# In-degrees counted from sorted destinations, and one histogram beside the aggregations of a graph network

## Time and profile before

| | us |
|---|---|
| median of 3 runs | 5533.93 (5531.75 to 5538.64) |
| span of the profiled execution | 6224.7 |
| set-up | 0 to 61 |
| input stage | 61 to 430 |
| first aggregation | 430 to 1609 |
| first dense stage | 1609 to 1726 |
| rows stage | 1726 to 1864 |
| second aggregation | 1864 to 3033 |
| second dense stage | 3033 to 3152 |
| mixing stage | 3152 to 3507 |
| dispatch and expert stage | 3507 to 4200 |
| the second layer | 4200 to 6225 |

### The profile page before, as it was taken

How to read it: one execution, slowest core, us unless ns; L and a number is a source line. 1 busy time by engine, 2 the same in 40 slices (tenths; PEclk the granted TensorE clock), 3 DMA queues, 4 the chain that set the end, 5 groups by cost and what they waited for, 6 DMA issues and landing times. The chain is left out here.

```text
span 6224.7 us, 73410 instructions
## 1 busy us (share of the span) xinstructions
PE 3894.4 (63%) x17328; PEld 2978.0 (48%) x17328; DVE 3162.7 (51%) x8327; ACT 2366.6 (38%) x6680; POOL 4026.6 (65%) x3591
## 2 busy tenths in 40 slices
PE   5645555555654555555756329987775877777763
PEld 4543343433453343333445228875554655556542
DVE  5544444444614444444578776535472435544566
ACT  2225566656425665666444213333441111111112
POOL 4876666666576666666588767875666666666523
PEclk7757777777776777777856569998997888889886
DMA  9774333333373333333378747868552112212235
GB/s 246 142 155 134 90 91 91 90 90 92 69 145 90 92 90 90 91 91 91 67 150 169 187 113 161 172 111 249 125 119 76 39 39 49 54 35 56 53 128 168
DMA packets 699733, 683.06 MB, mean 110 GB/s; under 512 B 96160, under 2 KB 623742, under 8 KB 698644
## 3 DMA queue, kind: packets, MB, share of 16 engines
q0 software_dynamic: 243744, 307.67, 25.2%
q1 hardware_dynamic: 440688, 345.82, 18.3%
q10 hardware_dynamic: 14980, 25.87, 1.2%
HBM read 475.03 MB, written 203.98 MB: 109 GB/s over the span
## 5 line engine op out<-in xcount | busy, mean ns | idle before, releaser
L729 POOL DMA_INDIRECT a_msg<-h_d,conv_src x1564 | 1479.0, 946 | 812.2 <-issue 437.0
L779 PE MATMUL a_part<-a_msg,a_pick 128*128 x3328 | 1226.9, 527 | 1046.6 <-issue 608.4
L621 POOL DMA_INDIRECT sums_d<-ss_total,ss_row_i x784 | 1276.5, 1628 | 452.1 <-issue 282.9
L779 PEld LDWEIGHTS a_part<-a_msg,a_pick 128*128 128x128 f32 x3328 | 819.5, 264 | 1415.1 <-issue 1271.6
L756 DVE TENSOR_TENSOR acc<-acc,a_part 128x256 f32 x1664 | 700.4, 421 | 1255.1 <-PE a_part L779 621.9
L3631 POOL DMA_INDIRECT es_edge<-gat_rows_d,el_idx x824 | 802.7, 974 | 473.4 <-issue 223.8
L743 DVE TENSOR_SCALAR a_pick<-ramp,conv_rel,conv_weight 128x128 f32<-128x128 f32 x1680 | 581.2, 347 | 0.2
L2581 ACT ACTIVATE cb_lent<-e_hp,e_b1c 128x256 f32<-128x256 f32 (+1 forms) x400 | 154.6, 469 | 1008.4 <-DMA gm_x<-in_L_gnn_z_out,gm_out_i 497.4
L2621 PE MATMUL e_yp<-cb_lent 128*128 128x256 f32 (+1 forms) x1568 | 417.0, 426 | 51.0 <-ACTq L2583 45.1
L2621 PEld LDWEIGHTS e_yp<-cb_lent 128*128 128x128 f32 (+1 forms) x1568 | 344.1, 221 | 116.7 <-ACTq L2583 47.1
L828 ACT ACTIVATE a1c_one_lo<-ramp,a1c_digits 128x128 bf16<-128x128 f32 x928 | 278.0, 387 | 311.0 <-remote 310.4
(11 more groups left out here) (557 smaller groups left out, 6851.0 us busy)
## 6 DMA issues: line engine op xcount, KB each, us to landing
ss_key_row<-keys_d SPq DMA_DIRECT2D x98, 512.0 KB
ss_pay<-in_edge_attr SPq DMA_DIRECT2D x97, 512.0 KB
a_msg<-h_d,conv_src POOLq DMA_INDIRECT x1564
experts_d<-cb_lent SPq DMA_DIRECT2D x96, 256.0 KB
cb_lent<-experts_d SPq DMA_DIRECT2D x30, 512.0 KB
y_rows_d<-node_h SPq DMA_DIRECT2D x28, 512.0 KB
e_xs<-y_rows_d SPq DMA_DIRECT2D x56, 256.0 KB
out_rows_d<-e_ys SPq DMA_DIRECT2D x56, 256.0 KB
```

The source lines that it names most:

```text
L621: nc.gpsimd.indirect_dma_start(self.out_d[q], bass.IndirectOffsetOnAxis(ap=self.row_i[n % 4][:, j:j + 1], axis=0), self.total[n % 4][:, j, ...
L729: nc.gpsimd.indirect_dma_start(msg[:, ds((j + PART) % SLOTS * C, C)], None, table, bass.IndirectOffsetOnAxis(ap=src_i[:, j:j + 1], axis=0) ...
L779: nc.tensor.matmul(part[b % BANKS][:, 0:C], pick[s % AHEAD][:], msg[:, ds(slot, C)], start=True, stop=True).then_inc(summed, 1)
```

## The change

The histogram of the first layer's destinations leaves the aggregations; the other one is counted in 128 batches of 8 columns, one per window, from a single set of buffers. PE's two numbers per step are packed into one, which it takes apart by masking. The in-degrees are found in the rows stage by the new class `InDegrees`: the sorted destinations lie as 112 rows of 896 keys; for each tile of 128 nodes, DVE marks which row holds a node's end (`choose`), PE brings that row's keys in two halves (`find`), and DVE counts the keys below the node (`count`); at the end a shift by one node and a subtraction give the degrees (`place`, `shift`). Each aggregation issues six of the edge sum's scatters behind its last gather. The dense stages serve seven groups, four of them behind blocks 1, 4, 7 and 10, and the mixing stage 20. `list_dst_digits` goes. `scatter_chunks` is `scatter` with its limits in chunks.

```diff
@@ EdgeOrder.set_up
-                nc.vector.tensor_scalar(self.chunk_row[:, :, 0], chunk_from[:], (SLOTS - 1) * C, None, ALU.bitwise_and)
-                nc.vector.tensor_scalar(self.chunk_row[:, :, 1], chunk_from[:], (PART * C).bit_length() - 1, None,
+                nc.vector.tensor_scalar(self.chunk_row[:, 0, :], chunk_from[:], (SLOTS - 1) * C, None, ALU.bitwise_and)
+                nc.vector.tensor_scalar(self.chunk_row[:, 1, :], chunk_from[:], (PART * C).bit_length() - 1, None,
                                         ALU.logical_shift_right)
+                dve.drain()
+                nc.vector.tensor_tensor(self.chunk_row[:, 0, :], self.chunk_row[:, 0, :], self.chunk_row[:, 1, :],
+                                        ALU.add)
@@ aggregate
         @block.scalar
         def _(act):
-            def window(n, i, h):
-                counts.scalar_batch(act, h % 2, i * 2 + h // 2)
-            over_windows(act, W, window)
+            with act.Fori(0, WINDOWS) as n:
+                counts.scalar_batch(act, n)
...
+            sums.scatter_chunks(pool, group * sums.B, group * sums.B + AHEAD_CHUNKS)
...
-            regs = [pe.alloc_register(f"{tag}_{what}{b}") for b in range(K) for what in ("slot", "in")]
+            regs = [pe.alloc_register(f"{tag}_chunk{b}") for b in range(K)]
-                pe.reg_load(regs, chunk_row[0:1, ds(n * K, K), :])
-                slots = [pe.snap(r, min_val=0, max_val=(SLOTS - 1) * C) for r in regs[0::2]]
-                parts = [pe.snap(r, min_val=1, max_val=PARTS) for r in regs[1::2]]
+                pe.reg_load(regs, chunk_row[0:1, 0, ds(n * K, K)])
+                where = [pe.snap(r, min_val=1, max_val=(SLOTS - 1) * C + PARTS) for r in regs]
...
-                    pe.wait_ge(landed, parts[b] & 255)
-                    slot = slots[b]
+                    pe.wait_ge(landed, where[b] & 255)
+                    slot = pe.snap(where[b] & (SLOTS - 1) * C, min_val=0, max_val=(SLOTS - 1) * C)
...
-                counts.tensor_batch(pe, h % 2, i * 2 + h // 2)
+                counts.tensor_batch(pe, n)
@@ CountBeside
-    BATCHES = 64
+    BATCHES = 128
...
-        self.digits = [sb(f"digits{q}", [P, 2, B], F32) for q, B in enumerate(self.cols)]
-        self.one_lo = [sb(f"one_lo{q}", [P, B, P]) for q, B in enumerate(self.cols)]
-        self.one_hi = [sb(f"one_hi{q}", [P, B, NHI]) for q, B in enumerate(self.cols)]
+        self.digits = sb("digits", [P, 2, B], F32)
+        self.one_lo, self.one_hi = sb("one_lo", [P, B, P]), sb("one_hi", [P, B, NHI])
@@ new
+class InDegrees:
+    ROW = EdgeOrder.PER * P
+    ROWS = CE // EdgeOrder.PER
+    HALF = ROW // 2
...
+    def load(self, sp):
+        rows = self.keys_d[:, 1, :].rearrange("(p b) e -> p b e", b=EdgeOrder.PER)
+        keys = self.keys[0:self.ROWS, :].rearrange("p (b e) -> p b e", e=P)
+        sp.dma_start(keys, rows).then_inc(self.keys_in, 16)
+        sp.wait_ge(self.next_ready, 1)
+        sp.dma_start(self.next[0:self.ROWS - 1, :], rows[1:self.ROWS, 0, 0:2]).then_inc(self.keys_in, 16)
+    def prepare(self, dve):
...
+        dve.wait_ge(self.keys_in, 32)
+        nc.vector.tensor_tensor(self.first[0:R], self.first[0:R], self.keys[0:R, 0:1], ALU.min)
+        nc.vector.tensor_copy(self.whole[0:R], self.keys[0:R])
+        dve.drain()
+        for to, of in ((self.firsts, self.first), (self.nexts, self.next)):
+            nc.vector.tensor_scalar(to[0:R], ramp[0:R, 0:NT], -float(P), of[0:R, 0:1], ALU.mult, ALU.add)
+        for digit, by, op in ((0, 127, ALU.bitwise_and), (1, (NHI - 1) * P, ALU.bitwise_and)):
+            keys = self.keys.bitcast(I32)
+            nc.vector.tensor_scalar(keys[0:R, :], self.whole[0:R], by, None, op)
+            dve.drain()
+            nc.vector.tensor_copy(self.digits[digit][0:R, 0:self.ROW], keys[0:R, :])
+            dve.drain()
...
+    def choose(self, dve, t):
+        R, ramp, behind = self.ROWS, self.k.ramp[0:self.ROWS, :], self.behind[t % 2]
+        self.nc.vector.tensor_scalar(behind[0:R], ramp, self.nexts[0:R, t:t + 1], None, ALU.is_le)
+        dve.drain()
+        if t >= 2:
+            dve.wait_ge(self.offered, 2 * t - 2)
+        self.nc.vector.scalar_tensor_tensor(self.chosen[t % 2][0:R], ramp, self.firsts[0:R, t:t + 1], behind[0:R],
+                                            ALU.is_gt, ALU.mult).then_inc(self.chose, 1)
+    def find(self, pe, t):
+        R, H = self.ROWS, self.HALF
+        pe.wait_ge(self.chose, t + 1)
+        for half in (0, 1):
+            if t:
+                pe.wait_ge(self.taken, 2 * t + half - 1)
+            for digit in (0, 1):
+                mm = self.nc.tensor.matmul(self.found[half][:, 0:H + half], self.chosen[t % 2][0:R, :],
+                                           self.digits[digit][0:R, half * H:half * H + H + half],
+                                           start=digit == 0, stop=digit == 1)
+            mm.then_inc(self.offered, 1)
+    def count(self, dve, t):
+        nc, H = self.nc, self.HALF
+        for half in (0, 1):
+            dve.wait_ge(self.offered, 2 * t + half + 1)
+            if half:
+                nc.vector.tensor_copy(self.at[:, 1, t:t + 1], self.found[1][:, H:H + 1])
+            nc.vector.tensor_scalar(self.junk[:], self.found[half][:, 0:H], self.node[:, t:t + 1], 0.0, ALU.is_lt, ALU.add,
+                                    accum_out=self.counted[:, half, t:t + 1])
+            dve.drain().then_inc(self.taken, 1)
...
@@ constants
-MIX_GROUPS = 22
+MIX_GROUPS = 20
-DENSE_GROUPS = 6
+DENSE_GROUPS = 7
+AHEAD_CHUNKS = 6
@@ dense_and_norms
         def served(n):
-            return all_groups[n * early // blocks:(n + 1) * early // blocks]
+            return all_groups[n // 3:n // 3 + 1] if n % 3 == 1 and n // 3 < early else ()
...
-            sums.scatter(pool, first - 2, first + DENSE_GROUPS - 2)
+            sums.scatter_chunks(pool, (first - 2) * sums.B + AHEAD_CHUNKS, (first + DENSE_GROUPS - 2) * sums.B)
...
-                if n == 5:
-                    sums.make_equal(dve, first + 2, first + 2)
-                    sums.choose_rows(dve, first, first)
-                if n == 10:
-                    sums.make_equal(dve, first + 3, first + 3)
-                    sums.choose_rows(dve, first + 1, first + 1)
+                if n % 3 == 0 and 0 < n <= 3 * early:
+                    g = all_groups[n // 3 - 1]
+                    sums.make_equal(dve, g + 2, g + 2)
+                    sums.choose_rows(dve, g, g)
...
-                sums.make_equal(dve, g + 1, g + 1)
-                if n == 0:
-                    sums.choose_rows(dve, g - 1, g - 1)
+                sums.make_equal(dve, g + 2, g + 2)
                 sums.choose_rows(dve, g, g)
-            sums.make_equal(dve, first + DENSE_GROUPS, first + DENSE_GROUPS)
@@ rows_from_channels
         @block.vector
         def _(dve):
-            for g in range(first, first + ROWS_GROUPS):
+            degrees.prepare(dve)
+            degrees.choose(dve, 0)
+            def tile(t, b, r):
+                if t + 1 < REAL_T:
+                    degrees.choose(dve, t + 1)
+                degrees.count(dve, t)
+            def serve(g):
                 sums.make_equal(dve, g + 1, g + 1)
                 sums.choose_rows(dve, g - 1, g - 1)
+            each_tile(tile, serve)
+            degrees.place(dve)
...
+                degrees.find(pe, t)
...
+            degrees.shift(pe)
...
+            degrees.load(sp)
```

More of the change, by code:

```diff
@@ L606, in scatter, with scatter_chunks @@
     def scatter(self, pool, first, last):
+        self.scatter_chunks(pool, max(first, 0) * self.B, last * self.B)
+    def scatter_chunks(self, pool, first, last):
         nc, B, Q = self.nc, self.B, self.Q
-        for chunk in range(max(first, 0) * B, last * B):
+        for chunk in range(first, last):
             n, j = divmod(chunk, B)
@@ L656, in _, with aggregate @@
             nc.vector.tensor_tensor(start[:], tile_start[:], within[:], ALU.add)
-def aggregate(k, tag, table, src_i, rel, weight, first_row, chunk_row, freed_row, acc, counts, first_batch, clear=None):
+def aggregate(k, tag, table, src_i, rel, weight, first_row, chunk_row, freed_row, acc, counts, first_batch, sums, group,
+              clear=None):
     nc = k.nc
@@ L780, in window, with __init__ @@
                                      ).then_inc(summed, 1)
[L781 removed]
+                counts.tensor_batch(pe, n)
             for n in range(WINDOWS):
[L783 removed]
+                window(n)
             counts.tensor_end(pe)
 class CountBeside:
[L789 to L793 removed]
+    BATCHES = 128
+    def __init__(self, k, lo, hi, count):
+        self.k, self.nc, self.lists, self.count = k, k.nc, (lo, hi), count
+        self.cols = lo.shape[1] // self.BATCHES
     def open(self, c, tag, first):
[L797 removed]
+        nc, B = self.nc, self.cols
         self.first = first
@@ L833, in scalar_batch @@
             nc.scalar.activation(whole, whole, ACT.Relu, bias=self.k.ones[:, 0:1], scale=-1.0)
```

(38 more changed lines are left out.)

119 lines of the change are left out of this document (74 added, 45 removed).

## The result

The changed kernel takes 5576.55 us in the median of four runs (5572.93 to 5582.09), the kernel before 5536.28 beside it (5531.75 to 5541.69): a ratio of 1.0076, 95% interval 1.0064 to 1.0089, so 40 us or 0.76% slower. The forecast was +26.5 us and slower. The sign held and so did the whole range, but the median lies 4.5 us above the likeliest case's own range of 5546 to 5572. Two of the forecast's terms were wrong in size (the six scatters and mixing), and a third, the rows stage, came out right for another reason than the one given.

The account below looks back on a forecast made before the run. The prediction took the unprofiled aggregations as bound by POOL's gathers, not by the profile's stall. Terms 10 + 8.5 + 14 - 6 = +26.5 us on 5533.9 gave 5560.4 us, +0.5%; range 5492 to 5592, likeliest case 5546 to 5572.

Parts of the forecast that it names:

- Histogram at 0: Aggregations: dropping one histogram gains 0 us, since PE and ACT work lies beside POOL's gathers, 15.3 us a window.
- Six scatters at +10: Aggregation ends: six scatters behind the last gather cost 5 us, twice, +10 us (between 0 and +22).
- the end moves by 11.2 - 6 = 5 us: Each aggregation's end: six scatters take 11.2 us, some 6 us hidden while PE trails the gathers.
- Dense stages at +8.5: Dense stages: seven groups in the chain of PE, ACT and DVE cost +4.2 us each, +8.5 (between 0 and +12).
- Rows stage at +14: Rows stage with degrees: 149 us against 138 by DVE's sum, +11, plus 3 for lock step (bounds 0 and +35).
- lock step: Rows stage: PE and DVE wait for each other each half, +3 us; as a rival +35 instead of +14, 5581 us, 15%.
- the last choice it needs falls near 132 us: Rows stage: POOL's last needed choice of rows comes near 132 us, eight scatters of 15 us follow, so POOL ends with DVE.
- The port lock: Rival, rows stage: DVE's first comparisons lock POOL out of the shared port, up to 17 us more, 5577 us, 6%.
- Mixing at -6: Mixing stage with 20 groups: two pairs of tiles lose 3.1 us each, -6 us (bounds 0 and -30).
- PE as the holder of the aggregations: Rival: PE's window still holds the unprofiled aggregations, and the shorter window gives 61 us back, -34, 5500 us, 25%.
- The 61 us that had no place: Part of the 691 us between profile and unprofiled runs left unplaced, perhaps lost to PE's window, 30 us per aggregation.
- Only POOL counts: Rival: mixing gives back its 30 us and the six scatters are hidden, -7 us, 5527 us, 12%.

Follow-up runs that it names:

- one_histogram: Kernel before with its first histogram's batches left out in both aggregations, on ACT and PE, in-degrees set to 1.0: 5534.56 us, ratio 1.0003.
- the second profile: Kernel before, unchanged, profiled once more: 5531.7 us, span 5529.9 us where the first profile had 6224.7.
- Seven_seven: Kernel before with seven groups in each dense stage, seven instead of nine in the rows stage, 22 in mixing: 5509.69 us, ratio 0.9957.
- six_rows: Kernel before with seven groups in each dense stage, six in the rows stage, 23 in mixing: 6256.35 us, ratio 0.9954; repeated 6189.08 us, 0.9948.
- no_ahead: Changed kernel with no scatters behind the last gather, the dense stages doing all 56: 5549.19 us, ratio 1.0032 to the kernel before.
- no_degrees: Changed kernel without finding the degrees in the rows stage, in-degrees set to 1.0: 5563.07 us, ratio 1.0054 to the kernel before.
- twice_after: Changed kernel with every product of the aggregations issued twice: 5570.03 us, ratio 1.0073 to the kernel before.
- dense_seven: Kernel before with the changed kernel's distribution alone (seven groups per dense stage, 20 in mixing), both histograms kept: 5535.70 us, ratio 1.0011.
- three_ahead: Changed kernel with three scatters behind each last gather instead of six: 6355.21 us, ratio 1.0104 to the kernel before; repeated 6255.56 us, 1.0046.

## Why the prediction was right, and where it was wrong

**The aggregations' bound: right, for a reason that was half wrong.** One_histogram and the second profile show the gathers as the bound, 782 x 1.25 us, in the runs that count. But the stall of the earlier trace rows is not made by the profile and does not follow PE's bursts of short products. Seven_seven has all the bursts and a span of 5502.6; six_rows has the stall in its profile, and all its other runs are as slow, 6240 to 6284 us. It is read from PE's sequencer, where I had not looked. Before each product PE masks a number for its wait on `landed` (line 775); this instruction in the second profile of the kernel before, then in the first one (duration ns, min, median, max):

```profile
L775 PEldq ALU_OP  x1664: 32/32/39, 446.3 to 2677.9; - x185
```
```profile
L775 PEldq ALU_OP  x1664: 2/32/1396, 449.3 to 3029.5; - x185
```

In the first profile one in ten of these, and of the waits on line 778, took some 0.7 us. The reading "only POOL counts in the aggregations" would have stood on firmer ground from this row.

**Histogram at 0: right**, and its cover is now measured, 2.5 us of room a window. The prediction bracketed PE's window between 11.5 and 14.4 of 15.3, so room between 0.9 and 3.8. It took PE's load at its shortest, 2.10; the median of the second profile is 6.14 and of the changed kernel 3.10, so the load gives back 3.0 us a window and not 1.0. None of it reaches the windows' length; only the end of the stage feels it, as the next part shows.

**Six scatters at +10: mis-sized, +20 to +23.** The step that failed is "the end moves by 11.2 - 6 = 5 us". The 6 us by which PE trails the last gather were right (DVE's last copy is at 1435.84, 6.7 us behind it). But POOL trails it too: from the last gather's end to the end of its drain are 6.4 us, in the first profile too (1582.30 to 1588.72). So in no_ahead POOL's drain and DVE's last copy end within 0.1 us of each other (1432.16 and 1432.09), and nothing of the six could be hidden: 13.0 and 12.8 us against no_ahead. In the kernel before DVE ends last, 2.3 us behind POOL's drain (1433.58 and 1431.28). With PE's shorter windows it trails the gathers less. The rest of the change gives back 3.7 and 2.3 us (992.3 and 986.0 in no_ahead, 996.0 and 988.3 before), and this end is 2.3 of the first and all of the second. The upper bound, +22, was the answer.

**Dense stages at +8.5: +5.7 to +6.5.** The chain behaves as forecast: up to the end of ACT's last instruction the stages grow by 3.8 and 5.1 us (4.2 each were forecast). The part missing is the same drain of POOL, which closed the stages of before 1.8 us after everybody else and no longer does.

**Rows stage at +14: +13.8, by another route.** DVE takes 2.35 us a tile (forecast 2.4), as the first comparisons of two tiles show in its timeline,

```profile
1642.27 0.32 DVE L923 TENSOR_SCALAR rc_in_behind<-ramp,rc_in_nexts 112x128 f32<-112x128 f32 x1
...
1644.62 0.29 DVE L923 TENSOR_SCALAR rc_in_behind<-ramp,rc_in_nexts 112x128 f32<-112x128 f32 x1
```

and by its waits (us in total, times, longest) it stood 1.6 us for PE's products in the whole stage, so lock step and its 3 us were not there:

```profile
DVE rc_in_junk L950 <- PE rc_in_found L938: 1.6, 2, 1.4
```

Its last work is done 147 us after the start, near the 149 forecast. But DVE does not end the stage. POOL does, with 137 us of scatters as before and one gap of 13.98. The failing step is "the last choice it needs falls near 132 us": the choice that costs is the first one, at the sixth tile. That the gap and DVE's excess have the same size is chance. The port lock, a rival at 6% by the rule of the Trainium skill ("SBUF — State Buffer", on the shared port pair), shows as at most 2 us: the mean of the 72 scatters is 1610 ns here, 1583 in no_degrees and 1595 in the kernel before, and no gap follows the first comparisons.

**Mixing at -6: -1 to -3.5.** The direction and its bound, DVE's chain, are right; a pair that loses its group loses less than the 3.1 us between the two pitches of the earlier trace rows. The step that failed is this price. The stage itself scatters: it takes 353.8 to 356.0 us in the profiles with 22 groups near 5530 us, and 350.3 to 352.7 in those with 20, so the means differ by some 3 us.

**The sum.** Forecast 10 + 8.5 + 14 - 6 = 26.5; by the two profiles 19.8 + 5.7 + 13.8 - 1.1 = 38.2. The excess is the scatters behind the gathers, +10, and mixing, +5, less 3 in the dense stages.

**Rivals.** PE as the holder of the aggregations is refuted by one_histogram and by twice_after. The 61 us that had no place were no hint of it: between the two profiles of the kernel before, the aggregations differ by 350 us and not 380, the last long stage by 296 and not 250, and four late stages by 50. The lock step falls with DVE's waits. "Only POOL counts" is refuted in mixing by dense_seven, and holds in the rows stage.

## What to carry to other kernels

Ask of each stage not only which engine computes last but which reports last: in the stages told of here POOL's queue needs 4 to 7 us behind its last indirect DMA before the barrier, so DMAs added "behind the last gather" were wholly on the path where POOL was the bound. Work taken off an engine is worth nothing as long as that engine has room. Doubling its work tests the room, if one reads the granted clock beside it: here it rose from 0.76 to 0.88 and from 0.77 to 0.95. A helper's units should go where another one costs least: a group of eight scatters costs 12 to 16.5 us where POOL is the bound and 3.3 where it isn't, and moving two of them was worth more than all else tried here.

Not tried: choosing the first group's rows ahead of the degrees. As an estimate from the trace, POOL's gap would close and DVE's 147 us would be the stage's end, up to 10 us less than 157.0.

## What the runs showed of the hardware that was not expected

The same kernel stands at 5530 us on one occasion and at 6218 or 6286 on another, with no profile. The two slow occasions were on two other chips than the fast ones, so chip and occasion can't be told apart. What differs in the traces is the sequencer of PE, and in part SP's: in three_ahead 361 of PE's 3969 register operations (`ALU_OP`) and 40 of SP's 477 took over 0.4 us, and none of DVE's and ACT's over 0.06. The mask ahead of the wait on `landed` takes 32 ns in the median of the changed kernel's profile and 39 at most, and up to 1409 in three_ahead's.

```profile
L761 PEldq ALU_OP  x1664: 32/32/39, 445.9 to 2708.1; - x185
```
```profile
L761 PEldq ALU_OP  x1664: 2/32/1409, 445.3 to 3135.9; - x185
```

The changed kernel has one such instruction more for each product, the mask that gives the slot. That may be why three_ahead stood at 1.0104 and 1.0046 of the kernel before there, with nothing of its scatters on the path; no run separates it: its first aggregation was 1210.8 us against 1186.2 in six_rows on the same chip, and 1180.9 against 1167.8 the second time. What makes these instructions slow stays open. Moving groups out of the rows stage pays at both levels, 0.43% with seven left there at 5530 us and 0.46 to 0.52% with six at 6218 and 6286.

A register costs PE 0.24 us to load in the median (6.14 us for 26, 3.10 for 13) and 0.08 at the shortest, from a source in SBUF; in the first profile of the kernel before the median was 0.18 (4.76 us for 26). The Trainium skill ("Runtime: NRT & Kernel Launch", instruction fetch mechanics) has about 200 ns a register for `TENSOR_LOAD`, which it tells of as a load from HBM. The medians here come near it; the shortest loads are far below.
